# Layer 0 keeps its normalised tokens transposed, makes its keys in three joint groups, and shares the PSUM banks out anew

## The reference

```python
x  = L0_attn_x                                   # (8, 256, 128)
xn = _layernorm(x)
x  = x + _L0_attn_ref(xn, ...) + _L0_ffn_ref(xn, ...)
xn = _layernorm(x)
x  = x + _L1_attn_ref(xn, ...) + _L1_ffn_ref(xn, ...)
# layer 0 attention: 16 query heads, 4 key/value heads of width 8, full softmax over 256 keys
scores = einsum('bghnd,bhsd->bghns', q, k);  attn = softmax(scores / 8 ** 0.5)
out    = einsum('bghns,bhsd->bghnd', attn, v);  out @ Wo + bo
# layer 0 second branch: relu(xn @ w1) @ w2, times a gate made from the two best of 8 logits xn @ Wg
# layer 1 first branch: in-projection, 4-tap convolution, silu, a scan over time with 16 states, gate
# layer 1 second branch: silu(a) * b, two 512 x 512 layers with gelu, one 512 -> 128
```

## Time and profile before

| | |
|---|---|
| median of 3 runs | 371.38 us (370.75 to 372.19) |
| profiled execution: span from first to last instruction | 370.3 us |
| busy share of the span: PE, ACT, DVE, POOL | 98%, 85%, 82%, 64% |
| first M, last M | 12.6 us, 139.2 us |
| first E, last E | 35.4 us, 187.6 us |
| first scan, last scan | 159.5 us, 356.5 us |

### The profile page before, as it was taken

The page is one execution under the profiler, slowest core; times in us unless marked ns, Lnnn a source line. Parts: engine busy times, 40 slices in busy tenths (PEclk is TensorE's granted clock), DMA queues, the critical chain, the costliest instruction groups (busy, mean ns, idle before and its releaser), DMA issues.

```text
span 370.3 us, 5874 instructions
## 1 busy us (share of the span) xinstructions
PE 361.6 (98%) x1810; PEld 185.9 (50%) x1810; DVE 303.1 (82%) x508; ACT 314.4 (85%) x540; POOL 238.0 (64%) x287
## 2 busy tenths in 40 slices
PE   7999999999999999999999999999999999999996
PEld 6757454546454553433324445465445464464546
DVE  4786879978788888579878768989999989998950
ACT  4934878886988887899998899999999999799870
POOL 2156504642527211342989673999999999999990
PEclk9999999999999999999969999999999999999999
DMA  6477282746265220220000000001000000000000
GB/s 217 125 145 147 93 200 35 174 143 120 58 110 123 43 55 2 52 85 0 1 21 3 1 0 2 0 0 48 5 0 21 0 3 28 1 2 1 0 28 28
DMA packets 29902, 19.63 MB, mean 53 GB/s; under 512 B 4496, under 2 KB 28848, under 8 KB 29616
## 3 DMA queue, kind: packets, MB, share of 16 engines
q1 hardware_dynamic: 29872, 19.26, 21.3%
HBM read 13.69 MB, written 5.37 MB: 51 GB/s over the span
## 4 chain that ended last, share of the span: by engine, by line
PE 68%; ACT 8%; DMA 2%; issue 2%; DVE 2%; SPq 0%; POOL 0%; ACTq 0%; DVEq 0%; POOLq 0%
PE bank L908 15%; PE bank L896 13%; PE bank L357 6%; PE bank L980 4%; PE bank L342 4%; ACT da L1088 3%; PE bank L869 3%; PE bank L885 3%; PE bank L886 3%; PE bank L953 3%; PE bank L933 3%; PE bank L388 2%; PE bank L328 2%; PE bank L396 2%; PE bank L970 2%; ACT pt L548 2%
## 5 line engine op out<-in xcount | busy, mean ns | idle before, releaser
L1218 POOL TENSOR_TENSOR acc<-acc,hb 128x512 f32<-128x512 f32 x128 | 158.1, 1273 | 11.6 <-DVE hb L1163 11.2
L1163 DVE TENSOR_TENSOR_SCAN hb<-da,bank 128x512 f32<-128x512 f32 x128 | 145.9, 1200 | 15.1 <-PE bank L869 9.1
L589 DVE TENSOR_REDUCE mx<-bank 128x2 f32<-128x512 f32 x128 | 83.1, 683 | 16.9 <-PE bank L328 14.4
L1088 ACT ACTIVATE da<-dt,nega 128x510 f32<-128x510 f32 x128 | 82.2, 713 | 0.2
L548 ACT ACTIVATE pt<-bank 128x512 f32<-128x512 f32 x128 | 71.2, 596 | 9.8 <-PE bank L342 8.7
L896 PE MATMUL bank<-sil,ld 128*128 128x512 f32 x128 | 59.1, 595 | 0.0
L908 PE MATMUL bank<-gelu,ld 128*128 128x512 f32 x128 | 58.5, 593 | 0.1
L342 PE MATMUL bank<-q_st,k_st 51*128 51x512 bf16 x128 | 42.2, 386 | 1.8 <-ACT pt L548 1.5
L328 PE MATMUL bank<-k_st,q_st 48*128 48x256 bf16 x240 | 38.9, 273 | 0.1
L896 PEld LDWEIGHTS bank<-sil,ld 128*128 128x128 f32 x128 | 24.3, 192 | 26.3 <-issue 25.7
L908 PEld LDWEIGHTS bank<-gelu,ld 128*128 128x128 f32 x128 | 23.8, 190 | 25.6 <-issue 24.7
(11 more groups left out here) (148 smaller groups left out, 534.0 us busy)
## 6 DMA issues: line engine op xcount, KB each, us to landing
q_st<-q_scr SPq DMA_DIRECT2D x8, 384.0 KB, 4.9
q_st<-q_scr SPq DMA_DIRECT2D x15, 192.0 KB, 3.8
ld<-in_pack SPq DMA_DIRECT2D x2, 1024.0 KB, 6.3
q_scr<-qk_parts SPq DMA_DIRECT2D x8, 192.0 KB, 2.1
k_st<-k_scr SPq DMA_DIRECT2D x15, 96.0 KB, 4.5
q_scr<-qk_parts SPq DMA_DIRECT2D x8, 128.0 KB, 2.1
out<-x SPq DMA_DIRECT2D x8, 128.0 KB, 1.9
ld<-in_pack SPq DMA_DIRECT2D x1, 968.0 KB, 5.4
```

What stands on the lines that cost most here:

```text
L589: eng.tensor_reduce(mx[:, 2 * pair:2 * pair + 2, q], s_bank[n % 2][:, :].rearrange("p (h k) -> p h k", h=2), AX.X, ALU.max).then_inc(mx_ok, 1)
L1088: act(da(n)[:, :, 1:T], dt[:, g % 2, c, :].rearrange("p (b n) -> p b n", b=GB)[:, :, 1:T], ACT.Exp, scale=nega[:, c, s:s + 1]).then_inc(da ...
L1163: eng.tensor_tensor_scan(hb[:, s % NPAIR, c, :], da(n).rearrange("p b n -> p (b n)"), b_bank(g, s)[:, :], 0.0, ALU.mult, ALU.add).then_inc ...
L1218: TT(acc[:, g % 2, c, :], acc[:, g % 2, c, :], hb[:, s % NPAIR, c, :], ALU.add).then_inc(add_ok, 1)
```

## The change

Arithmetic and results stay the same. What differs:

1. **Tokens kept.** `xnT` holds all 8 batches (in layer 1's buffer), and `xn` has two buffers, so tokens can be transposed long before they are used.
2. **Keys in three groups**: batch 0, batches 1 to 3, batches 4 to 7. `project_keys` puts each batch of a group at its own 32 output columns of the array; `k_out`, `split_k`, `put_keys` then work once for a group. `q_out`, `split_q`, `put` handle the queries alone. Semaphores of fetches and rows are split by parity of the batch.
3. **16 probability tiles** for each batch (8 new ones lie in layer 1's `hb`), and 4 value buffers.
4. **Three banks for each score product**: S in banks 0, 1, 5 and A in 2, 3, 6. S(n) waits for M(n-3), A(n) for E(n-3).
5. **The rest in two banks.** Bank 4 (`bP`) holds in turn the four `pv` of a batch, its `heads`, and both steps of `ffn_in` and `ffn_out`. Bank 7 (`bX`) has a half for tokens, queries and keys, and a half for values, maxima, `back` and `proj_out`. The strings `X_AFTER` ... `H_AFTER` say whose emptying each use waits for.
6. **All orders new**, 28 `warm` in place of 44, and 41 table loads on ACT in place of 49.

```diff
-NWARM = 44
+NWARM = 28
+NV = 4
+KEYS = ((0,), (1, 2, 3), (4, 5, 6, 7))
...
+T_AFTER = "v3 p0 q6 m5 p3 m7 p5 p6"
+F_AFTER = "- f0 f1 h1 h2 f4 h3 h4"
+O_AFTER = "f2 h0 f3 f5 f6 f7 h5 h6"
+H_AFTER = "o0 o1 o2 o3 o4 o5 o6 o7"
...
-    s_bank, st_bank = banks[0:2], banks[2:4]
-    pv_bank = banks[4]
-    bA, bB, bC = banks[5:8]
+    s_bank, st_bank = (banks[0], banks[1], banks[5]), (banks[2], banks[3], banks[6])
+    bP, bX = banks[4], banks[7]
+    half0, half1 = bX[:, 0:T], bX[:, T:2 * T]
...
+    def score_free(eng, b, n):
+
+        if b < LAST:
+            reached(eng, mx_ok, b, NH, n - 2)
+        else:
+            reached(eng, mx_ok, b, NH, n - 1 if n > 1 else (-2, 0)[n])
...
+    def emptied(eng, before, n):
+
+        name = before.split()[n]
+        if name == "-":
+            return
+        for signal, per in EMPTIED[name[0]]:
+            eng.wait_ge(signal, per * (int(name[1:]) + 1))
...
-            reached(eng, p_ok, b, NH, n - 1 if b < LAST else n)
+            reached(eng, p_ok, b, NH, n - 2 if b < LAST else n)
...
             if grp == 0:
-                reached(eng, o_ok, b, 1, 0)
+                emptied(eng, O_AFTER, b)
                 reached(eng, v_ok, b, 1, 1)
             at = VS * (1 - gp)
             for kv in range(NKV):
-                last = mm(pv_bank[kv * VW:(kv + 1) * VW, :], v_sb[b % 2][:, kt, kv, at:at + VW],
-                          pt[:, (4 * grp + kv) % 8, :], start=(grp == 0), stop=(grp == 3))
+                last = mm(bP[kv * VW:(kv + 1) * VW, :], v_sb[b % NV][:, kt, kv, at:at + VW],
+                          prob(b, 4 * grp + kv), start=(grp == 0), stop=(grp == 3))
             last.then_inc(pv_ok, 1)
...
+        def project_keys(j):
+            reached(eng, xnT_ok, KEYS[j][-1], 1, 1)
...
+            for i, b in enumerate(KEYS[j]):
+                last = mm(key_bank(j)[32 * i:32 * i + 32, :], wk4[:, 0:NKV * HD], xnT[b], start=True, stop=True)
+            last.then_inc(k_ps, 1)
...
             if n % 4 == 0:
-                reached(eng, pv_ok, b, 4, n // 4 - 1)
-            act(pt[:, n % 8, :], st(b, n)[:, :], ACT.Exp, scale=HD ** -0.5).then_inc(p_ok, 1)
+                reached(eng, pv_ok, b - 1, 4, n // 4 + 1)
+                if b == LAST and n >= 8:
+                    reached(eng, pv_ok, b, 4, n // 4 - 1)
+            act(prob(b, n), st(b, n)[:, :], ACT.Exp, scale=HD ** -0.5).then_inc(p_ok, 1)
```

More of the change, by code:

```diff
@@ L72 @@
 ORDERS = dict(
[L73 to L95, removed]
@@ L119 @@
-    gpsimd="""ones G qk_split G biased 6*G qk_split maxima_split 6*G biased 2*G qk_split maxima_split 6*G maxima_split
-        qk_split 3*G biased 7*G maxima_split qk_split 8*G maxima_split qk_split 7*G maxima_split G qk_split G
-        constants 7*G shifted maxima_split 8*G maxima_split split 2*start 3*add start 9*add split 9*add start 7*add
-        shifted 4*add 2*y start 9*add split 23*add start 2*y 2*add start 2*add split add start 27*add 2*y 32*add 2*y""",
+    sync="""x_in head x_in ffn_weights constants0 put x_in put_keys put 2*put_keys put fetch 2*put_keys put put_keys
+        2*put fetch stack rows put 2*rows 2*put fetch loads stack 2*put rows put put_keys 2*rows fetch 2*put put_keys
+        put loads stack 2*rows put_keys rows put fetch stack 2*rows put rows loads put fetch 3*put stack fetch 2*rows
+        put 3*rows put rows stack put fetch stack 3*rows stack loads 3*rows 2*b_rows out b_rows 2*out b_rows 5*out
+        landed""",
@@ L123 @@
+    gpsimd="""2*biased G ones split_k split_q 7*G split_q maxima_split 8*G split_q G maxima_split 7*G split_q split_k
+        maxima_split biased split_q 8*G maxima_split 6*G split_q 2*G maxima_split split_q 15*G maxima_split G
+        constants shifted G maxima_split 7*G maxima_split start split start 7*add split 2*start 22*add shifted 3*add
+        2*y start 8*add start 5*add split 19*add 2*y 3*add split 25*add start 2*add start add y 2*add y 31*add 2*y""",
 )
@@ L214, in layer0, with prob, score_bank, group_of @@
     LAST = NB - 1
-    def head_bank(b):
-        return bA if b < LAST - 1 else bC
+    NS3 = LAST * NH
     def st(b, n):
-        return st_bank[n % 2 if b < LAST else 0]
+        return st_bank[(b * NH + n) % 3 if b < LAST else 0]
+    def prob(b, n):
+        return pt[:, n % 8, :] if n < 8 or b == LAST else pt_more[:, n - 8, :]
+    def score_bank(b, n):
+        return s_bank[(b * NH + n) % 3 if b < LAST else (n + 1) % 2]
+    def score_free(eng, b, n):
[3 more added lines that the diff above has]
+            reached(eng, mx_ok, b, NH, n - 1 if n > 1 else (-2, 0)[n])
+    def group_of(b):
+        return next(j for j, batches in enumerate(KEYS) if b in batches)
+    def key_bank(j):
+        return half0 if j == 2 else st_bank[1][:, 0:T]
+    EMPTIED = dict(x=((xnT_ok, 1),), q=((q_ok, 1),), k=((k_ok, 1),), v=((v_ok, 1), (srt_ok, TPB)), m=((negm_ok, 1),),
+                   t=((oT_ok, 1),), p=((x1_ok, 1),), h=((on_ok, 1),), f=((y_ok, 1),), o=((o_ok, 1),))
+    def emptied(eng, before, n):
[4 more added lines that the diff above has]
+            eng.wait_ge(signal, per * (int(name[1:]) + 1))
+        if name == "q0":
+            eng.wait_ge(q_split, 1)
+            eng.wait_ge(kx_ok, 2)
     def x_part(b):
@@ L302, in ffn_weights @@
             eng.dma_start(w12[:, :], a["w12"]).then_inc(ld_ffn, 16)
-        return dict(x_in=x_in, head=head, constants0=constants0, ffn_weights=ffn_weights, put=put, fetch=fetch, rows=rows,
+        return dict(x_in=x_in, head=head, constants0=constants0, ffn_weights=ffn_weights, put=put, put_keys=put_keys, fetch=fetch, rows=rows,
                     stack=stack, loads=loads)
@@ L382, in ffn_in @@
                 reached(eng, xnT_ok, b, 1, 1)
[L383 removed]
+                emptied(eng, F_AFTER, b)
             else:
@@ L450, in warm @@
             for _ in range(2):
-                last = mm(pv_bank[:, 0:256], warm_in[:, 0:P], warm_in[:, P:3 * P], start=True, stop=True)
+                last = mm(st_bank[2][:, 0:256], warm_in[:, 0:P], warm_in[:, P:3 * P], start=True, stop=True)
             if n == NWARM - 1:
@@ L1179, in clear @@
                 settled(eng, done["st_ps"], (NB - 1) * NH)
-                settled(eng, done["stk_ok"], 32 * NB)
+                for p in range(2):
+                    settled(eng, done["stk_ok"][p], 16 * NB)
                 settled(eng, done["y_ok"], NB)
```

364 lines of the change are left out of this document (203 added, 161 removed).

## The result

The changed kernel takes 374.48 us (median of 6 runs, 373.3 to 376.66) against 371.58 us (6 runs, 369.79 to 372.19): a ratio of 1.0087, 95% interval 1.0064 to 1.011. It is slower by 0.9%; the forecast was 363.4 us. The profiled execution took 373.3 us with a span of 371.5.

A forecast was written before the change was run, and what follows sets the result against it. Bounds: bank coupling of DVE and ACT through PE until 140 us, ACT until 188, then PE. 10.4 - 4.0 + 0.6 + 2.0 - 1.0 = 8.0 us off 370.3, plus 1.1: 363.4 us; forecast band 359.5 to 367.5, range 357 to 371.

The forecast's parts named there:

- 140 us and later: From 140 us to the end: both stages shift and keep their length; 0 to 3.0 us won, taken as 0.
- a stage behind the last E that is longer than 184 us, if D, scan or add there come later against PE: Sign of a wrong forecast, from the last E to the end; 183 us was expected there.
- Slower than before, by the same bank: Rival: queueing at bank 4 makes a batch 16.2 us, 375.0 us in all; chance 0.12.
- Third bank +10.4: 36 to 140 us: a third bank for S and A shrinks M's gaps, 10.4 us won, bounds 0 and 11.9.
- bundles -4.0: Before 140 us: four bundles of three or four `pv` starve DVE, 5.4 us of gaps at most, 4.0 taken.
- +0.6 for ACT: Before 140 us: ten fewer q and k copies spare ACT 4.7 us; 0 to 2.4 us won, 0.6 taken.
- M waits for S under 5 us: Sign of a right forecast, in the stage that matches 36 to 140 us; M waited 11.9 us before.
- Start +2.0: Batch 0's scores before the first A: three banks win, the moved stack may cost; -1 to +3.2 us, 2.0 taken.
- Lag of E -1.0: End of layer 0's M's: three more E's of 0.6 us remain; 0 to 1.8 us lost, 1.0 taken.
- Shared bank 4: Rival: a batch's turns through bank 4 become the bound, 15.2 us a batch, 367.8 us in all; chance 0.12.
- The clock: Rival: fewer warm pairs lower PE's clock in the first 30 us, 364.6 us; inside the forecast's range, no own chance.

The follow-up runs named there:

- short adds: Four of POOL's group 2 adds on 64 of 512 columns: 371.5 us against the changed kernel's 374.5, 365.14 us against 365.5 with the old tail.
- the old tail: Changed kernel up to the end of layer 1's group 0, the order of the kernel before behind it on every engine: 365.47 us, ratio 0.9836.
- the new tail: The changed kernel's orders of layer 1's groups 1 to 3; put on the kernel before, with its old layer 0: 380.0 us, ratio 1.0234.
- Four versions that removed one or both: Changed kernel with `split` later on POOL, 371.9 us; also two scans earlier on DVE, 372.83; also b 35 to 39 earlier on PE, 373.17; b 39 to 41 moved again, 371.91.

## Why the prediction was wrong

The step that failed is "140 us and later": "both stages shift and keep their length", and behind them "0 to 3.0 us won; I take 0, since PE's work is the same". The same work took 189.0 us from the last E to the end against 182.1. With the old order on the same layer 0 it takes about 181 us (spans of 363.5 to 363.7 less a last E that ends at 182.9 in the trace of that order with short adds), so the step would have held for an unchanged order. What the prediction did not ask is whether the new order of groups 1 to 3 keeps POOL fed: it read PE's 179.04 of 182 us in the earlier trace rows and passed over POOL's 158.97 in the same row, which from 232 to 356 us has no idle time above 0.3 us, and it costed point 6 of the change (all orders new) by counting pieces. Its own sign of being wrong, "a stage behind the last E that is longer than 184 us, if D, scan or add there come later against PE", names what happened, but no term of the sum and no rival had a price for it. The rival "Slower than before, by the same bank" gives 375.0 us, close to the measured 374.5 by luck: it needs batches of 16.2 us, and they take 14.8.

The other steps, in the order of the sum:

- *Third bank +10.4 and bundles -4.0, +0.6 for ACT.* Batch 0's last M to the last M is 103.8 us against 110.0: 6.2 us, forecast 7.0. A batch takes 14.8 us against the 14.5 forecast and 15.7 measured before. In sign and sum right. The two terms apart can't be had: taken out alone a bank costs four to five times what I gave both less the bundles (27 and 34 us to 6.4), because the order around it is another, and a bundle taken apart gains nothing.
- *Bundles*: I gave four bundles 5.4 us of gaps at most; the trace has 6.75 us beside them, 1.94 of these behind a wait for POOL's gate sum, so 4.81 us behind S. The sign "M waits for S under 5 us" did not come: 7.7 us.
- *Start +2.0*: first A at 33.9 us in place of 35.0, 1.1 us.
- *Lag of E -1.0*: 7.3 us ahead at the last M, 5.7 at the last E: -1.6 us.
- *Shared bank 4*: the rival fell. `heads` waits 1.6 us in 5 pieces for `o_out` over seven batches. E's 4.9 us and `o_out`'s 5.1 us of waiting for `pv` may contain more of it.
- *The clock*: the fall came at 322 us, not in the first 30, behind a wait, not a cause of its own: with the old tail the mean is 1.00. Of the fall at 185 us in the kernel before I wrote that it agrees with a rule on idleness; PE's longest wait there is 0.71 us, so it agrees only in that PE was less busy.

Layer 0 and an order that fits it give 371.6 - 365.5 = 6.1 us where the sum said 8.0. The 9 us on top are the new tail's. Of these, 6.7 us lie in group 2's order and up to 2.3 in group 1's, some of which may belong to the joint. POOL's idle times of 3.34 and 4.39 us are the visible part of the 6.7, and the run with short adds shows that POOL's string sets the end. Four versions that removed one or both got back 1.3 to 2.6 us. In the three of them with a trace to read, the stall moved on: to b on PE, then to the wait for the last y and the clock that it costs. Which single piece of group 2's order is out of place stays open, and so does what makes POOL 2.6 us later at the end of group 1 (265.7 against 263.1 us); its idle 3.33 us at 220.5 us is a candidate that was not tried.

## What to carry to other kernels

When a change moves a stage earlier, check for each engine behind it how full it is from where on, not over the whole stage: an engine at 87% of a stage (POOL here) can be full for two thirds of it, and an order that leaves it idle there has nothing later to make it good from. When an order was rewritten for a new resource, cut both orders at a point where they hold the same work and run each half with the other's; two runs told here more than any look at the trace. A long bundle beside an idle engine may be what covers the hole: look at what the third engine does in that moment before pulling it apart.
